# Attention scores as three fp32r terms in row halves of the array, in place of six bf16 terms over all rows

## The reference

```python
qkv = (x @ Wqkv).reshape(b, l, 3, H, DH)          # H = 16 heads of DH = 16
q, k, v = qkv[:, :, 0], qkv[:, :, 1], qkv[:, :, 2]
q = q * cos + rotate_half(q) * sin
k = k * cos + rotate_half(k) * sin
attn = softmax(einsum('bqhd,bkhd->bhqk', q, k) * DH ** -0.5)
x = layernorm(x + einsum('bhqk,bkhd->bqhd', attn, v).reshape(b, l, d) @ Wo)
x = layernorm(x + ffn(x))   # ffn: RMS norm, a shared MLP, and two of eight expert MLPs per token
```

## Time and profile before

| | us |
|---|---|
| runs | 1295.58, 1291.84, 1294.05 (median 1294.05) |
| span of the profiled execution | 1291.3 (no other time is given for it) |
| TensorE busy | 1224.3 (95%) |
| TensorE weight loads | 934.5 (72%) |
| VectorE busy | 976.6 (76%) |
| ScalarE busy | 996.4 (77%) |
| GpSimd busy | 583.9 (45%) |

### The profile page before, as it was taken

The page is one execution under the profiler, slowest core; times in us unless marked ns, Lnnn a source line. Parts: engine busy times, 40 slices in busy tenths (PEclk is TensorE's granted clock), DMA queues, the critical chain, the costliest instruction groups (busy, mean ns, idle before and its releaser), DMA issues. The chain is left out here.

```text
span 1291.3 us, 29542 instructions
## 1 busy us (share of the span) xinstructions
PE 1224.3 (95%) x9440; PEld 934.5 (72%) x9440; DVE 976.6 (76%) x1925; ACT 996.4 (77%) x2043; POOL 583.9 (45%) x590
## 2 busy tenths in 40 slices
PE   4899999999999999979899969999999999999997
PEld 3444444444444444337899969999999999999897
DVE  6888887888788888728676648777777777777596
ACT  6699998999899999846654437777777777777687
POOL 6332322232223220005467745666666666666763
PEclk8899999999999999988899979999999999999999
DMA  9300000010000000433022246777777777776363
GB/s 298 117 19 19 18 19 20 2 35 3 19 2 19 2 18 3 144 104 117 18 91 100 87 158 197 260 251 253 246 238 238 235 249 253 253 239 217 101 218 119
DMA packets 125414, 161.28 MB, mean 125 GB/s; under 512 B 17088, under 2 KB 108224, under 8 KB 125312
## 3 DMA queue, kind: packets, MB, share of 16 engines
q1 hardware_dynamic: 118496, 141.25, 33.7%
q0 software_dynamic: 6816, 18.75, 4.1%
HBM read 122.06 MB, written 37.52 MB: 124 GB/s over the span
## 5 line engine op out<-in xcount | busy, mean ns | idle before, releaser
L546 DVE TENSOR_REDUCE att_mx<-att_psA 128x1 f32<-128x512 f32 x512 | 337.8, 683 | 75.5 <-PE att_psA L331 74.9
L461 ACT ACTIVATE att_prob<-att_psB 128x512 f32<-128x512 f32 x512 | 299.7, 600 | 54.0 <-PE att_psB L341 41.0
L341 PE MATMUL att_psB<-att_qk 128*128 128x512 bf16 x512 | 197.6, 388 | 12.8 <-issue 5.6
L1648 ACT ACTIVATE exp_psU<-exp_psU,ew_b 128x256 f32<-128x256 f32 x312 | 126.6, 447 | 103.7 <-PE exp_psU L1605 103.7
L331 PE MATMUL att_psA<-att_qk 96*128 96x512 bf16 x512 | 196.9, 386 | 3.0 <-DVE att_mx L546 3.0
L1699 DVE CAST exp_hh<-exp_psU 128x512 fp32r<-128x512 f32 x156 | 107.9, 692 | 101.9 <-ACT exp_psU L1648 101.9
L1588 PE MATMUL exp_psD<-exp_w2h,exp_hh 128*128 128x256 f32 x624 | 175.8, 282 | 0.0
L1603 PE MATMUL exp_psU<-exp_xh,exp_w1h 128*128 128x256 f32 x624 | 173.7, 278 | 1.4 <-DVE exp_xl L1690 1.4
L1605 PE MATMUL exp_psU<-exp_xh,exp_w1l 128*128 128x256 f32 x624 | 173.4, 278 | 0.0
L1604 PE MATMUL exp_psU<-exp_xl,exp_w1h 128*128 128x256 f32 x624 | 173.3, 278 | 0.0
L1589 PE MATMUL exp_psD<-exp_w2l,exp_hh 128*128 128x256 f32 x624 | 172.4, 276 | 0.0
(11 more groups left out here) (215 smaller groups left out, 3244.9 us busy)
## 6 DMA issues: line engine op xcount, KB each, us to landing
ew_w<-ew SPq DMA_DIRECT2D x40, 1024.0 KB, 6.1
exp_w<-ew SPq DMA_DIRECT2D x38, 1024.0 KB, 5.8
slots_x<-pre_acc SPq DMA_DIRECT2D x13, 780.0 KB, 10.8
pre_spare<-slots_x SPq DMA_DIRECT2D x39, 260.0 KB, 4.1
out_g<-rows_y SPq DMA_DIRECT2D x32, 256.0 KB, 4.1
ew_b<-eb SPq DMA_DIRECT2D x39, 128.0 KB
pre_spare<-xT SPq DMA_DIRECT2D x8, 512.0 KB, 4.5
attn_rows<-att_ob SPq DMA_DIRECT2D x8, 512.0 KB, 2.8
```

Source lines behind the costliest of these rows:

```text
L341: pe.matmul(psB[B_BANK[n % U]][:, :], r[:, 1, kt * P:(kt + 1) * P], r[:, 0, :], start=True, stop=True).then_inc(s_bmm, 1)
L461: act.activation(prob[:, n % PR, :], psB[B_BANK[n % U]][:, :], ACT.Exp, scale=SCALE).then_inc(s_exp, 1)
L546: dve.reduce_max(mx[:, g % 2, n % U:n % U + 1], psA[A_BANK[n % U]][:, :], AX_X).then_inc(s_max, 1)
```

## The change

- Each of q and k is two fp32r pieces (`PIECES = 2`), high and low, and three products of pieces are kept: `TERMS = 3`, 48 rows for score rows. Two more rows carry the two pieces of the negated maximum (50 rows, `KM`).
- Two heads lie one above the other: `stack` holds pairs, the even head's terms in columns 0 to 47, the odd one's in 64 to 111. One turn makes both (`turn_pair`, fp32, four per group in place of eight bf16 ones), and `copy_pair` copies 112x512. The even head's operands then lie in partitions 0 to 49 and the odd head's in 64 to 113.
- A step issues score rows first, then score columns, and `COLS_ORDER` puts the two in opposite halves.
- Two banks for `psA`, three for `psB`.
- The maxima are turned in fp32 and split after the turn by two VectorE instructions on 16x128; four DMAs place them.
- For token tiles after the first four, VectorE only copies Q/K out of PSUM (`copy_qk`); GpSimd does the rope, both pieces, and also the splitting of x, whose high part ScalarE made. The first four tiles are turned by VectorE and their high pieces made by ScalarE.
- `QK_LEAD` is 7 and not 6, `T_LEAD` 41 and not 29, the turn of the maxima stands at step 9 and not 10. Some buffers lie in space of a later stage.

The core of the diff:

```diff
-    TERMS = 6
+    TERMS = 3
     KR = TERMS * DH
+    KM = KR + 2
+    PAIR_COLS = 64 + KR
...
-    QK_LEAD, V_LEAD = 6, 4
+    QK_LEAD, V_LEAD = 7, 4
-    T_LEAD = A_LEAD + 5
-    PIECES = 3
+    T_LEAD = A_LEAD + 17
+    TURNS = 4
+    PIECES = 2
-    Q_PIECES, K_PIECES = (1, 1, 1, 2, 2, 3), (1, 2, 3, 1, 2, 1)
+    Q_TERMS, K_TERMS = ((0, 1), 2), ((0, 2), 1)
+    COLS_ORDER = (1, 0, 3, 2)
+    ROWS_ORDER = (0, 1, 2, 3)
...
-        A_BANK = [0, 1, 2] * 5 + [1]
-        B_BANK = [0, 1] * 8
+        A_BANK = [0, 1] * 8
+        B_BANK = [0, 1, 2] * 5 + [1]
...
+        def rows_of(g, i, j, n):
+
+            first = 64 * (j % 2)
+            return qk[first:first + n, g % RING, i, j // 2, :]
...
             def place_max(g, it):
 
                 wait(sp, it, s_mev, g + 1, 1)
-                for k in range(PIECES):
-                    sp.dma_start(qk[96 + k:97 + k, g % RING, 0, :, :].rearrange("o j (t c) -> o (j t) c", c=P),
-                                 mrow[k * U:(k + 1) * U, g % 2, :]).then_inc(s_mld[g % 2], 16)
+                for half in range(2):
+                    for k in range(PIECES):
+                        r = 64 * half + KR + k
+                        sp.dma_start(qk[r:r + 1, g % RING, 0, :, :].rearrange("o j (t c) -> o (j t) c", c=P).bitcast(F32),
+                                     mrow[half * 2 * NT:(half + 1) * 2 * NT, k, :].bitcast(F32)).then_inc(s_mld[g % 2], 16)
...
+            def split_x(b, it):
+
+                v = 16 * (b // 2 + 1)
+                pool.wait_ge(s_x[b % 2], v if it is None else v + it * 16)
+                wait(pool, it, s_vmm, NT * (b - 1), 1)
+                pass_on(xt[:, b % 2, 0, 0:2])
+                pool.tensor_copy(xh[:, b % 2], xt[:, b % 2]).then_inc(s_xh, 1)
...
+            def split_hi(tile, it):
+                b, t = tile // NT, tile % NT
+                if t == 0:
+
+                    wait(pool, it, s_tmm, TURNS * HG * (b - 1), TURNS)
+                wait(pool, it, s_rr, tile + 1, 1)
+                pass_on(rr[:, tile % 2, 0:2])
+                for i in range(2):
+                    for half, cols in enumerate(halves(b, t, i)):
+                        pool.tensor_copy(hi_terms(cols, i), twice(of_half(rr[:, tile % 2, :], i, half))).then_inc(s_hi, 1)
...
+                    if valid(n + A_LEAD, NG * U):
+                        score_rows(n + A_LEAD, it)
                     if valid(n, NG * U):
                         score_cols(n, it)
-                    if valid(n + A_LEAD, NG * U):
-                        score_rows(n + A_LEAD, it)
...
+            def copy_qk(tile, it):
+
+                wait(dve, it, s_qmm, tile + 1, 1)
+                wait(dve, it, s_rr, tile, 1)
+                dve.tensor_copy(xc, psX[:, :]).then_inc(s_qrd, 1)
```

More of the change, by code:

```diff
@@ L298, in period, with split_lo @@
+            def split_lo(tile, it):
+                b, t = tile // NT, tile % NT
+                for i in range(2):
+                    for half, cols in enumerate(halves(b, t, i)):
+                        wait(pool, it, s_hi, 4 * tile + 2 * i + half + 1, 4)
+                        pool.tensor_tensor(lo_term(cols, i), of_half(rr[:, tile % 2, :], i, half), term(cols, 0).bitcast(F32),
+                                           ALU.subtract).then_inc(s_stk, 1)
             def period(p, it):
@@ L318, in _ @@
-            groups(pool, period)
+                if valid(tile, NT * B):
+                    if tile >= FILL:
+                        turn_pairs(tile, it)
+                        split_hi(tile, it)
+                    split_lo(tile, it)
+                b = (tile + 1) // NT
+                if (tile + 1) % NT == 0 and valid(b - 2, B - 2):
+                    split_x(b, it)
+            groups(pool, period, passes=PASSES - 1)
         @block.tensor
@@ L354, in turn_head, with turn_pair @@
+            def turn_pair(k, it):
+                g, pair, i = k // TURNS, k % TURNS // 2, k % 2
+                b = g // HG
+                wait(pe, it, s_tev, k, TURNS)
+                if k % (TURNS * HG) == 0:
+                    wait(pe, it, s_stk, 4 * NT * (b + 1), 4)
+                if it is None and k == 0:
+                    pe.wait_ge(s_init, 7)
+                    pe.wait_ge(s_const, 5)
                 for t in range(NT):
-                    m = pe.transpose(psT[0:KR, half, t * P:(t + 1) * P], stack[:, b % 2, t, half, h % H, :], ident[:, :])
@@ L494, in x_hi @@
-            def x_hi(b, it):
-                v = 16 * (b // 2 + 1)
-                act.wait_ge(s_x[b % 2], v if it is None else v + it * 16)
-                wait(act, it, s_vmm, NT * (b - 1), 1)
+                act.wait_ge(s_rr, tile + 1)
+                for i in range(2):
+                    for half, cols in enumerate(halves(b, t, i)):
+                        act.activation(hi_terms(cols, i), twice(of_half(rr[:, tile % 2, :], i, half)), ACT.Copy).then_inc(s_hi, 1)
+            def x_hi(b):
+                act.wait_ge(s_x[b % 2], 16)
@@ L633, in _ @@
             dve.wait_ge(s_tab, 32)
[L635 to L644 removed]
             def period(p, it):
[L647 to L650 removed]
+                if valid(p + QK_LEAD, FILL):
+                    first_rope(p + QK_LEAD)
                 for u in range(U):
```

294 lines of the change are left out of this document (116 added, 178 removed).

## The result

The changed kernel takes **1326.71 us** (median, 1323.71 to 1330.73), the one before 1294.11 (1291.84 to 1295.58): a ratio of 1.0265, 95% interval 1.0236 to 1.0293. It is slower by 33 us, where 47 us less was forecast; 1326.71 lies outside the range of 1224 to 1300.

What follows compares the result with a forecast made beforehand. TensorE's own work was taken as the bound: 12.7 + 1.1 shapes + 0.6 banks = 14.4 us a group. 25 x 1.6 = 40, + 7.5 at the end, + 3 start, - 3.5 late x = 47 us less: 1247 us, range 1224 to 1300.

Steps and rivals of the forecast that it cites:

- Entering and leaving the half-array shape: TensorE, nine more full-shape blocks between half-shaped pairs: 9 x 0.12 = 1.1 us a group, bounds 0 and 2.2.
- the price of a pair among blocks: TensorE, score rows and columns overlap wholly: 0.235 us a pair, 16 x 0.235 = 3.8 us in place of 6.9.
- a pair of 0.37: TensorE's pair cost from which the group reaches the old 16.0 us: 8.9 + 1.1 + 16 x 0.37.
- rival 1: TensorE: the halves don't overlap, a pair costs 0.47 us; 1338 us, or about 1305 without shape prices; 13%.
- banks: Score rows with two banks, not three: TensorE waits for VectorE's maxima at short steps, 0.6 us a group.
- A lower granted clock in attention: Closing caveat: it would void the sum, which uses rows at 2.4 GHz; no size or chance given.
- Start: 3 us less: Start of attention: a shorter fill, partly taken back by more lead and serial turns; 3 us gained, bounds 0 and 6.
- the sign named: Sign that the forecast is right: the head of the first score columns is near 49 us.
- GpSimd's chain: GpSimd's rope and splits per token tile: 7.0 to 8.6 us, 10.6 to 13.5 with x's split every fourth tile.
- a late x: GpSimd's x split ends 0.6 us after TensorE needs it, 6 times: 3.5 us lost, bounds 0 and 13.
- rival 3: Four DMAs placing the maxima take 5 us in place of 3.9; period some 15.3 us, 1270 us in all; 8%.
- Rival 2: TensorE: a pair's weight loads follow each other, pair 0.39 us, period 16.3 us, about 1298 us in all; 9%.

Runs made afterwards that it cites:

- the full shape: Changed kernel with both score matmuls contracting over partitions 0 to 111 for every head, so halves no longer overlap: 1311.66 us, ratio 1.0163 to the kernel before.
- the run of 1303.0: Changed kernel with pair turns moved to steps 0, 4, 8 and 12 and other blocks directly behind them: 1303.0 us, ratio 1.0088 to the kernel before.
- the bf16 run: Kernel before, still bf16, with both score matmuls contracting only over partitions 0 to 63: 1397.55 us, ratio 1.084 to the kernel before.
- the last run above: The run of 1303.0 with three banks for score rows and two for score columns: 1314.88 us, ratio 1.0182 to the kernel before.

## Why the prediction was wrong

**The step that failed most: "Entering and leaving the half-array shape", with the price of a pair among blocks.** The forecast took 9 x 0.12 = 1.1 us for shapes and 16 x 0.235 = 3.8 for pairs. The pairs take 6.5 us, 2.7 more, though they do start within 0.01 us of each other and the overlap gives 0.24 in a lone step, as forecast.

What was missing is what the neighbours cost. First, an fp32r score matmul directly behind a block costs 0.1 more, in the full shape too (0.34 and 0.23 in that run). The sign of it lay in the earlier trace rows: the first of the Q/K matmuls takes 0.31 to the next (313.89 to 314.20) and only those behind it 0.235. The forecast took the price of a matmul in the middle of a run of its kind, and 13 of the 16 pairs stand directly behind a block. Second, the half shape costs 0.1 more ahead of a block of full shape (0.33 and not 0.23, 432.93 to 433.26 against 300.73 to 300.96) and 0.2 more in the block itself (a turn 0.58 and not 0.35). That is some 0.3 for each of nine added blocks, 3.1 us a group by the estimate above with 0.3 of a wait for maxima in it; 1.1 was taken and 2.2 was the upper bound. The forecast's own mark for "slower", a pair of 0.37, was passed without rival 1's mechanism being true.

The Trainium skill ("TensorEngine Tiling (Array Packing)", Key Properties) says that a change of tiling mode drains the engine; the trace agrees, with loads that start at 304.15 and 304.73 together with their matmuls. The Trainium skill ("TensorE: Matmul & The Clock Gate", Part 2, Step-by-step) says that weight loads are pulled ahead of running matmuls when the row groups do not conflict or the load goes to the background buffer. The trace shows it in the full shape (0.23 us ahead) and not across a change of shape.

In the terms of the runs, the period of 14.4 becomes 16.6 as follows:

| | forecast | runs |
|---|---|---|
| full shape, one matmul behind the other | 12.7 + 3.8 = 16.5 | 17.0 |
| price of the half shape | +1.1 | +3.1 (1.9 measured, 1.2 estimated) |
| overlap | -3.8 | -3.5 (2.3 measured, 1.2 estimated) |
| banks | +0.6 | within the rest |
| period | 14.4 | 16.6 |

The 0.5 of the first line is 1.3 more for the scores (13 blocks, 0.1 each) and 0.8 less for the rest, mostly the turns (0.35 each and not 0.45) and P times V (1.00 and not 1.09). The forecast's own pieces add up to 12.8 and not 12.7, which changes nothing.

**The clock: named, not priced.** "A lower granted clock in attention would also void the sum" was the last sentence and had no chance of its own. It is worth some 14 us at the two ends (the run with full shape there). The step "Start: 3 us less" became 12.7 more: 9.8 of it is this clock, and with the clock up the first output turn is still 2.8 later than before (76.75 against 73.92); the cause of that stays open. The first score columns are at 60.29, where the sign named was near 49. At the second turn of the loop there is more: that group took 24.7 us and the next 18.1 at a granted 0.53, where the kernel before took 20.5 and 16.2. It begins with an idle TensorE, for which the profile names no releaser:

```profile
353.19 0.79 PE L384 MATMUL att_psA<-att_qk 48*128 48x512 f32 x1 [3.60 <-issue]
```

The kernel before has two such idle times, of 2.9 and 2.8 us (at 199.35 and 332.17). The run with full shape at the ends, whose loop is the changed kernel's, has one of 3.7 at the first turn and none at the second. So they differ between programs with the same loop, and no run tells why. With the clock behind them they make the 4 us in the loop of that run, and the 8 in the run of 1303.0.

**Banks.** 0.6 us was foreseen from two row banks. Undone in the changed kernel it gave 0.1, in the kernel before 0.55; the term is real, but in the changed kernel it hardly shows; that the shape changes hide it was not tested.

**Right.** ScalarE has slack (67 of 100 us). GpSimd's chain, forecast at 7.0 to 8.6 and with x's split 10.6 to 13.5, runs from 337.44 to 344.89 and to 348.48, so 7.4 and 11.0:

```profile
337.44 0.73 POOL L335 TENSOR_TENSOR pre_acc<-pre_acc,att_sin 128x256 f32<-128x256 f32 x1 [9.19 <-DVE pre_acc L624]
...
344.98 1.03 POOL L320 CAST att_xh<-pre_spare 128x1024 fp32r<-128x1024 f32 x1
346.09 2.39 POOL L323 TENSOR_TENSOR att_xl<-pre_spare,att_xh 128x1024 fp32r<-128x1024 f32 x1
```

It was in time, so the 3.5 us for a late x did not come; the copy of 1024 took 1.03 us, the lower bound, and not the 1.5 that the forecast gave beside it. The maxima's DMAs delayed TensorE once, by 4.6 us ahead of the last group (3.8 before), so rival 3 was rightly small. Rival 2 was wrong in mechanism, since both loads of a pair start together (304.73). That its period of 16.3, and rival 1's 16.5 without a price for shapes, come near the measured 16.6 is luck.

## What to carry to other kernels

Where blocks of another shape stand between row-tiled pairs, weigh the gain of each pair (here 0.24 us) against the price of each block that stands alone among them (here about 0.3 us in fp32r, 0.2 in the bf16 run). Here 16 pairs (3.5 us) and nine more blocks (3.1) nearly cancel. Price an operation by a row with the same neighbour ahead of it, never by its steady step. And if a change makes TensorE's matmuls use fewer rows, forecast the granted clock of each stretch as a term of its own, above all where the pipeline fills, drains or stalls.

## What the runs showed that was not expected

- A high busy share did not bring the clock up: with score matmuls of 48 and 50 rows TensorE was busy 99.89 of 100 us at a granted 0.50 for some 370 us. Yet in the changed kernel the clock, once up, stayed at 1.00 with 48-row halves in the loop. How late it comes up, to stay for 70 us or more, differs by shape and by run. In the five profiles with full shape at the start that is at 28.6 to 55.8 us, in the eight with half shape at 58.2, 65.0, 72.7, 72.9, 74.4, 80.2, 86.7 and 411.9. So the half shape goes with a later rise, but it does not fix it: the 58.2 is the last run above, granted 1.00 in 36 to 48 us. What decides stays open. The Trainium skill ("TensorE: Matmul & The Clock Gate", Part 1) says that activity releases the throttle; the trace agrees in so far as TensorE was active ahead of each rise, and shows beside it the 370 us of activity without one.
- With both matmuls of a step in one half, TensorE started the next step's rows, in the other half, ahead of this step's columns, which stand before them in its list: 429.35 against 429.65. The semaphores still came in the list's order (430.05 for the columns, 430.08 for the rows that had started first). This is what kept part of the overlap in the run that was to take it away.
- A pair directly behind a block is followed by the next pair after 0.34 us, with two or three banks alike. No run has a third pair in a row without a wait, so the step of a long run of pairs is not known.
- A longer group can be the faster kernel: 17.0 us a group with 1311.66 us in all, 16.6 with 1326.71.
